# Layer 0: the rounded rows of the ternary product turned as bfloat16, and GpSimd's two additions in the form with two operations

## What is computed

```
x = x + attention_0(layernorm(x), ctx_1024, mask)
x = x + ternary_ffn(layernorm(x))
x = x + attention_1(layernorm(x), ctx_1024)       # causal
x = x + gated_ffn(x)

def ternary_ffn(x, ternary_weight, bias, act_scale):
    scale = maximum(act_scale, 1e-05)
    x_int = clip(round(x / scale), -127, 127)
    w     = ternary_weight.astype(float32) - 1.0   # -1, 0 or 1
    return einsum('bsi,oi->bso', x_int * scale, w) + bias
```

## Time and profile before

| | |
|---|---|
| median of 3 runs | 1340.28 us (1339.98 to 1344.3) |
| the profiled execution | 1342.39 us |
| its span, first to last instruction | 1340.6 us |
| mean granted TensorE clock | 0.967 of full speed |
| TensorE products busy | 1237.0 us, 92% of the span |
| VectorE busy | 1031.7 us, 77% |
| ScalarE busy | 870.8 us, 65% |
| GpSimd busy | 517.4 us, 39% |

### The profile page before, as it was taken

How to read it: one execution, slowest core, us unless ns; L and a number is a source line. 1 busy time by engine, 2 the same in 40 slices (tenths; PEclk the granted TensorE clock), 3 DMA queues, 4 the chain that set the end, 5 groups by cost and what they waited for, 6 DMA issues and landing times. The chain is left out here.

```text
span 1340.6 us, 21785 instructions
## 1 busy us (share of the span) xinstructions
PE 1237.0 (92%) x7715; PEld 656.7 (49%) x7719; DVE 1031.7 (77%) x1772; ACT 870.8 (65%) x1483; POOL 517.4 (39%) x680
## 2 busy tenths in 40 slices
PE   9999899999999999999999999999998999970498
PEld 5565522334343443434555545545554785430298
DVE  5867688898888888886767788888774664996764
ACT  4455437676777777677665656665555666869693
POOL 3555401144453444445565433333334102647600
PEclk9999969999999999999999999999999999995699
DMA  8999774323344252433424563343201001326133
GB/s 280 378 326 329 274 174 120 105 64 94 93 118 128 64 138 80 113 99 102 129 78 116 147 179 92 105 122 83 80 18 49 1 0 47 141 94 244 70 110 111
DMA packets 88076, 170.84 MB, mean 127 GB/s; under 512 B 14743, under 2 KB 49311, under 8 KB 86431
## 3 DMA queue, kind: packets, MB, share of 16 engines
q1 hardware_dynamic: 87083, 167.37, 40.0%
q10 hardware_dynamic: 883, 2.05, 0.7%
HBM read 108.26 MB, written 60.31 MB: 126 GB/s over the span
## 5 line engine op out<-in xcount | busy, mean ns | idle before, releaser
L1409 DVE TENSOR_REDUCE b_neg_max<-b_score 128x1 f32<-128x512 f32 (+3 forms) x864 | 540.6, 662 | 139.4 <-PE b_score L896 71.9
L1145 ACT ACTIVATE b_probs<-b_exp 128x512 f32<-128x512 f32 (+1 forms) x864 | 467.5, 580 | 270.1 <-PE b_exp L920 267.2
L893 PE MATMUL b_score<-b_k_stack,b_q_stack 97*128 97x512 bf16 (+3 forms) x1024 | 355.6, 351 | 15.5 <-DVE b_neg_max L1409 9.7
L920 PE MATMUL b_exp<-b_q_stack,b_k_stack 100*128 100x512 bf16 (+3 forms) x1024 | 345.0, 342 | 6.6 <-ACT b_probs L1145 6.2
L941 PE MATMUL b_av<-b_probs,b_values 128*17 128x512 f32 (+3 forms) x2048 | 223.1, 519 | 1.2 <-POOL b_probs L1243 0.9
L893 PEld LDWEIGHTS b_score<-b_k_stack,b_q_stack 97*128 97x128 bf16 x1024 | 99.9, 98 | 242.8 <-DVE b_neg_max L1409 132.7
L920 PEld LDWEIGHTS b_exp<-b_q_stack,b_k_stack 100*128 100x128 bf16 x1024 | 100.1, 99 | 75.7 <-ACT b_probs L1145 23.0
L1243 POOL TENSOR_SCALAR_AFFINE_SELECT b_probs<-b_probs 128x512 f32<-128x512 f32 x96 | 61.5, 641 | 175.5 <-ACT b_probs L1145 175.4
L1259 POOL CAST b_max_parts<-b_neg_max 128x16 bf16<-128x16 f32 x64 | 12.8, 201 | 268.1 <-DVE b_neg_max L1409 265.8
L896 PE MATMUL b_score<-diag_qk,minus_big 128*128 128x128 bf16 x512 | 112.5, 220 | 0.0
L1697 PE MATMUL f_bank<-normed,f_w_upT 128*128 128x512 f32 x192 | 82.7, 592 | 0.0
(11 more groups left out here) (257 smaller groups left out, 2141.3 us busy)
## 6 DMA issues: line engine op xcount, KB each, us to landing
b_q_stack<-s_q SPq DMA_DIRECT2D x378, 64.0 KB
s_k<-a_part_k SPq DMA_DIRECT2D x48, 256.0 KB, 3.3
b_k_stack<-s_k SPq DMA_DIRECT2D x60, 192.0 KB
s_up<-f_up SPq DMA_DIRECT2D x6, 1536.0 KB, 5.1
s_va<-a_va SPq DMA_DIRECT2D x16, 544.0 KB, 5.3
b_values<-s_va SPq DMA_DIRECT2D x16, 544.0 KB, 4.3
a_mask_q<-mask_in SPq DMA_DIRECT2D x8, 1024.0 KB, 8.3
b_k_stack<-s_k SPq DMA_DIRECT2D x60, 128.0 KB
```

What stands on the lines that cost most here:

```text
L893: mm = pe.matmul(o, q, KS[half][0:R_MAX, h, 0:w], start=True, stop=causal or not general)
L920: mm = pe.matmul(o, k, QS[half][0:NSTACK, h, q0:T], start=True, stop=not masked)
L1145: nc.scalar.activation(probs[kc][:, h0:h0 + m, q0:T], exp_bank[n % RINGS][:, 0:m * w].rearrange("p (h n) -> p h n", h=m), ACT.Exp).then_in ...
L1409: nc.vector.tensor_reduce(neg_max[u][:, qt, h0:h0 + m], score_bank[n % RINGS][:, 0:m * w].rearrange("p (h n) -> p h n", h=m), AX.X, ALU.ma ...
```

## The change

- GpSimd adds MAGIC in the form of `tensor_scalar` with two operations, the second adding 0.0. A third pass takes MAGIC off again, in the same form, and writes the whole numbers as bfloat16 to XQ, which lies in a free half of the room of XQT.
- This pass waits for the turns of the batch before, which read XQ, and for the addition; `quantized` counts three a batch.
- TensorE turns XQ instead of XN, with the bfloat16 identity, into `work` seen as bfloat16.
- ScalarE's copy to XQT reads bfloat16 and has no bias; `less_magic` and its preset on VectorE are gone.

```diff
-        less_magic = sb("less_magic", [P, 1], F32)
...
+        XQ = normed[:, 7, TT * D // 2:TT * D].bitcast(BF16).rearrange("p (t d) -> p t d", t=TT)
+        work_b = work[:, :].bitcast(BF16)
...
-        PRESETS = 3
+        PRESETS = 2
...
                         if n == 4:
-                            pe.wait_ge(quantized, 2 * (b + 1))
-                        mm = turn(XN, n - 4)
+                            pe.wait_ge(quantized, 3 * (b + 1))
+                        for x in range(TT):
+                            mm = pe.transpose(work_b[:, x * P:(x + 1) * P], XQ[:, x, (n - 4) * P:(n - 3) * P], const["ident_b"][:, :])
...
-                    nc.scalar.activation(XQT[:, c, :], work[:, :], ACT.Identity, bias=less_magic[:, 0:1]).then_inc(by_act[0], 1)
+                    nc.scalar.activation(XQT[:, c, :], work_b[:, 0:T], ACT.Copy).then_inc(by_act[0], 1)
...
                     nc.gpsimd.tensor_scalar(XN, XN, 127.0, -127.0, ALU.min, ALU.max).then_inc(quantized, 1)
-                    pool.wait_ge(quantized, 2 * b + 1)
-                    nc.gpsimd.tensor_scalar(XN, XN, MAGIC, None, ALU.add).then_inc(quantized, 1)
+                    pool.wait_ge(quantized, 3 * b + 1)
+                    nc.gpsimd.tensor_scalar(XN, XN, MAGIC, 0.0, ALU.add, ALU.add).then_inc(quantized, 1)
+                    if b > 0:
+                        pool.wait_ge(after_full[0], NF[0] * (b - 1) + 6)
+                    pool.wait_ge(quantized, 3 * b + 2)
+                    nc.gpsimd.tensor_scalar(XQ, XN, -MAGIC, 0.0, ALU.add, ALU.add).then_inc(quantized, 1)
...
-            nc.vector.memset(less_magic[:, :], -MAGIC).then_inc(preset, 1)
```

## The result

The change makes the kernel slower: 1366.21 us in the median of 6 runs (1365.24 to 1369.12), against 1340.19 for the kernel before. The ratio is 1.0191, with a 95% interval of 1.0179 to 1.0203. I had forecast 1334.7, and a range that ended at 1339.5.

A forecast was written before the change was run, and what follows sets the result against it. TensorE was taken to bound layer 0's batches, busy 58.49 of 59.00 us. Turns 3.1, batch 0 0.27 and batch 7 2.2 summed to 5.6 us, so 1340.3 became 1334.7, range 1332.5 to 1339.5.

The forecast's parts named there:

- GpSimd's chain: GpSimd's passes over the quantized rows: two additions at 1.04 us each replace one of 2.79, ending the chain 0.56 us earlier.
- the sign: Whole kernel: the change was forecast to make it faster, chance 0.60; slower had 0.05, within the measurement's resolution 0.35.
- the slack of 3.00: Batch 1, with batches 2 to 6 alike: GpSimd's last pass ended 3.00 us before TensorE's turn.
- The last rival: GpSimd's addition is slow in any form, 2 x 2.79: chain 2.9 us later, batches 0 and 7 lose, 1344.6; chance 0.07.
- The turns: TensorE's transposes of the quantized rows, now bf16: 0.44 us saved a batch, 3.1 us for batches 0 to 6.
- Does the saved time last?: VectorE's unbroken block behind both turns: it starts 0.44 us earlier too, so the saving was counted whole.
- Batch 0 and batch 7: TensorE's waits for GpSimd: batch 0's turn 0.27 us earlier; batch 7's wait 2.15 becomes 1.59, gaining 2.2 with the clock held.
- the cap by the next cut: GpSimd's cut in batch 7 moves by only 0.56 us, limiting that batch's gain from 2.5 to 2.2 us.
- The clock at a wait of 1.6: TensorE's clock behind batch 7's shortened wait of 1.59 us: it holds, judged by waits of 0.92 and 1.66; worth 1.52.
- the first rival: The clock falls again in batch 7 behind the 1.59 us wait: gain only 4.4 us, time 1335.9; chance 0.25.
- The copies on ScalarE: ScalarE's 16 copies at L1111, now reading bf16 without bias: whatever they save is hidden behind other work.

The follow-up runs named there:

- e1: A program of its own, not an edit of the kernel: GpSimd passes over 1024 numbers a partition in twenty forms; min then max 1.04 us, addition alone 2.78.
- e6: The changed kernel with both GpSimd additions as add, then multiply by 1.0: 1336.68 us against 1342.16 for the kernel before, ratio 0.9962.
- e3: The changed kernel with both GpSimd additions in the form with one operation: 1348.07 us, ratio 1.0047 to the kernel before.
- e2: The kernel before, with only GpSimd's addition given a second operation adding 0.0: 1343.11 us against 1341.87, ratio 1.0009.
- e4: The changed kernel with one GpSimd pass, adding MAGIC and taking it off, in place of the two additions: 1342.35 us, ratio 0.9995 to the kernel before.

## Why the prediction was wrong

**GpSimd's chain.** This step failed, and with it the sign. I priced the additions at 1.04 by the clip's row, as the nearest in form, and held 1.54 and 2.79 for the upper bounds. They took 3.66 and 3.63. The bound was wrong in kind: I took the addition alone as the worst that an addition could cost, "if the addition is slow in any form, 2 x 2.79", and never let the second operation cost anything of its own. The rows did not show an addition with an addition. They showed min then max at 0.80 ns an element, one operation at 2.5, and add then multiply, which I read as 1.29 and which is 0.83 by the two lengths now known (0.554 us for 256, 1.19 for 1024 in e1); that two operations can be quicker than one was itself the warning that I had no rule for the price. The honest upper bound was the slow row plus what its second operation might add, 2.79 and more. From 2.8 us a pass on, the chain passes the slack of 3.00 that I had read and named; at 3.66 and 3.63 TensorE's turn is 1.8 late in each of five batches, and the time is not 1344.6 but 1366.21. That the price, and nothing else in the change, turned the sign is shown by e6: the same kernel with passes of 1.05 is 5 us faster than before.

The Trainium skill's rule, which I had set beside it (GPSIMD Engine Reference, section 3.1: a loop of at most two operations runs at 1.03 cycles an element, an estimated 0.88 us for 1024), is near to four pairs and the copy, 1.04 to 1.05 here, and to none of the other pairs nor any single operation.

**The last rival** had its mechanism right, in size and place, for its own price: with 2.79 twice (e3) batches 1 to 5 paid 0.1 each, batch 6 nothing, and batches 0 and 7 waited 3.00 and 5.07. Its time, 1344.6, was a little low against 1348.07 (6.2 above the kernel before of the same runs, where I had 4.3): I had let the middle batches' gain stand whole, 0.44, and it was 0.3.

**The turns.** Right: 0.22 and 0.24 after the two turns, where I had 0.24 and 0.26; 0.40 a batch in e6. The Trainium skill's 81 ns for a load and product in a sustained stream (TensorE: Matmul & The Clock Gate, "Back-to-back issue gap") is not what these runs of four show: four turns and the way to the next product in 0.22 are 55 ns each. My sum of 3.1 for batches 0 to 6 was 2.6 in e6 (its normalizing of batch 7 begins 2.87 earlier, 0.27 of it from batch 0): batch 6, whose turns lie in layer 1, gave only 0.26.

**Does the saved time last?** Nearly. VectorE's unbroken block moved with TensorE: in e6 the product that waits 0.20 for it begins 17.67 behind the first turn of batch 1, where it had begun 18.06 behind it. But the turns give 0.22 and 0.26, and only 0.40 of these 0.48 reach the next batch. In batch 1 the rest goes at 342.27, at the fourth product behind the second turn, where TensorE's weight load waits for ScalarE's exponentials. I had asked about VectorE alone.

**Batch 0 and batch 7** came out right for the chain that I had assumed, in e6: batch 0's turn is 0.27 earlier, as read from the start that was late in the earlier trace rows; batch 7's wait is 1.59, as worked out; the clock held; and the gain behind the turn was 1.62, where the cap by the next cut had left 2.2 - 0.56 = 1.64 (the cut ended at 686.90, the weighing began at 687.00). The whole was 5.0 in the trace and 5.1 by the ratio, where I had 5.6.

**The clock at a wait of 1.6.** Here I was right by luck. I had let one wait of 1.66 decide. In the changed kernel five waits of 1.61 to 1.66 were followed by the lower clock twice and not three times, and the 1.58 ahead of the gated part, which held before, lost it once in e6. Waits of 2.15 (before), 3.0 (e2, e3) and more always lost it in these traces. By these five waits the first rival's 0.25 was too little; but of all 22 waits of 1.57 to 1.67 between 250 and 1100 us in the eight traces of the kernel only these three were followed by the lower clock, so the runs don't settle the chance. Nor is one wait needed: the fall at 834 us in e4 came behind two waits of 0.43 and 0.79.

**The copies on ScalarE** fell from 0.676 to 0.591 us and nothing waited for them, before or after.

What stays open is why these four pairs alone are quick. No run shows it.

## What to carry to other kernels

Price an instruction of GpSimd by a row with the same operations in the same order, not by one with the same shape of operands; where there is none, measure it by itself before anything is built on it, and where a single operation is needed, try it with a neutral second one (multiply by 1.0 behind an addition: 1.05 us in place of 2.78, worth 2.7 us to this kernel by one edit). And when a slack is read off, ask what happens beyond it: a chain that repeats in every batch costs nothing up to its slack and everything, times the number of batches, past it, with the slow clock on top. So the upper bound of such a step must be pushed until it crosses the slack or a reason forbids it.

## What the runs showed of the hardware

- GpSimd, 1024 f32 a partition: min-max (in this order), add-multiply, multiply-add and multiply-multiply with immediates take 1.04 to 1.05 us, one operation alone 2.77 to 2.79, every other pair tried 3.62 to 3.66; add-multiply with the second number an immediate and the first from a column 1.11, both from columns 1.19, add-add from columns 3.78, one operation alone from a column 2.85. A bf16 output changes nothing.
- A wait of about 1.6 us of TensorE was followed by the lower clock in 3 of 22 cases and not in the others, at the same place and in the same program. The low stretch cost 1.5 and 1.6 us behind waits of 1.65 and 1.64, 1.5 behind one of 2.15, and 2.8 behind one of 4.69, as differences between the traces.
- Transposes of bf16 follow each other at 0.055 us with a load of 128 columns each, at a granted clock of 1.00.
